# Hybrid block kernel: two of the four masked q/k halves of the upper head groups move from the end of the first head group to the second, and one q rounding is taken ahead of a fold

## The reference, cut to what matters

```
qkv = (layernorm(x) @ Wqkv + bqkv)            # 16 heads of 16 features
q = q*cos + rotate_half(q)*sin ; k likewise
scores = q @ k.T / sqrt(16), causal
out = softmax(scores) @ v
```

## Time and profile before

| what | value |
|---|---|
| median of three runs | 1737.48 us (1735.87 to 1737.56) |
| the profiled execution: span | 1734.1 us |
| the profiled execution's own time | not listed apart; the three runs lie 1.8 to 3.5 us above its span |
| busy share of the span | PE 95%, DVE 55%, ACT 42%, POOL 39% |
| chain that ended last | PE 78%, DVE 11%, ACT 6%, no visible cause 3%, POOL 1% |
| mean granted TensorE clock | 0.98 of full speed |

### The profile page before, as it was taken

One profiled execution on the slowest core, in us unless ns is written; L12 is line 12 of the kernel. 1 busy time (PEld: TensorE's weight loads), 2 busy tenths in 40 slices (PEclk: granted clock), 3 DMA queues, 4 the chain that ended last, 5 costly groups with the idle time before them and its releaser, 6 DMA issues.

```text
span 1734.1 us, 40451 instructions
## 1 busy us (share of the span) xinstructions
PE 1652.0 (95%) x17108; PEld 1186.6 (68%) x17108; DVE 952.4 (55%) x1978; ACT 722.2 (42%) x1510; POOL 670.1 (39%) x851
## 2 busy tenths in 40 slices
PE   6589999999999999999999999999999999999998
PEld 3467458864688547884588756886478855787477
DVE  6864657356553656546574565636565365744621
ACT  4433462334632455234633346233552346433441
POOL 5733335343542426324263433524353242733110
PEclk9779999999999999999999999999999999999999
DMA  5110000000000000000000000000000000000000
GB/s 184 51 50 13 1 14 3 1 25 13 3 2 6 20 13 3 2 25 1 14 3 1 25 14 2 3 0 25 13 3 2 13 13 1 4 2 0 1 13 13
DMA packets 20387, 25.77 MB, mean 15 GB/s; under 512 B 1488, under 2 KB 18800, under 8 KB 20208
## 3 DMA queue, kind: packets, MB, share of 16 engines
q1 hardware_dynamic: 19872, 22.13, 4.0%
q0 software_dynamic: 336, 1.05, 0.2%
HBM read 18.98 MB, written 4.19 MB: 13 GB/s over the span
## 4 chain that ended last, share of the span: by engine, by line
PE 78%; DVE 11%; ACT 6%; issue 3%; POOL 1%; DMA 1%; SPq 0%; DVEq 0%; POOLq 0%; ACTq 0%
PE ring L1592 19%; PE ring L1606 18%; PE ring L1752 6%; PE attn_out L1772 5%; PE ring L1578 5%; PE ring L1710 3%; PE ring L1538 3%; PE ring L1732 3%; PE ring L1645 3%; PE ring L1735 2%; PE ring L1530 2%; PE ring L1755 2%; PE ring L1615 2%; DVE x_z_xb L1176 1%; DVE big L1266 1%
## 5 line engine op out<-in xcount | busy, mean ns | idle before, releaser
L1333 DVE TENSOR_REDUCE maxes<-ring 128x2 f32<-128x1024 f32 (+5 forms) x290 | 197.5, 739 | 86.4 <-PE ring L1735 85.6
L757 POOL TENSOR_TENSOR rstd<-mean_var,eps_and_power 128x2 f32<-128x2 f32 x96 | 19.3, 201 | 470.0 <-DVE mean_var L1170 470.0
L1606 PE MATMUL ring<-w_down,big 128*128 128x256 f32 x784 | 175.9, 379 | 0.0
L1606 PEld LDWEIGHTS ring<-w_down,big 128*128 128x128 f32 x784 | 147.3, 190 | 19.6 <-issue 0.4
L809 POOL TENSOR_TENSOR big<-big,decay_blocks 128x256 f32<-128x256 f32 x192 | 141.5, 766 | 40.5 <-issue 35.9
L780 POOL TENSOR_TENSOR mix<-mix,z_t 128x512 f32<-128x512 f32 x80 | 85.7, 1100 | 117.8 <-DVE mix L1222 117.8
L1752 PE MATMUL ring<-big 32*128 32x512 f32 (+3 forms) x1024 | 124.6, 472 | 0.9 <-DVE big L1365 0.9
L1266 DVE TENSOR_TENSOR big<-big,decay_blocks 128x256 f32<-128x256 f32 x192 | 123.8, 671 | 1.0
L1024 ACT ACTIVATE big<-ring,up_bias 128x256 f32<-128x256 f32 x196 | 82.1, 470 | 101.3 <-PE ring L1592 101.3
L1592 PE MATMUL ring<-maxes,w_mlp 128*128 128x256 f32 x512 | 118.2, 385 | 0.0
L1592 PE MATMUL ring<-maxes,w_up 128*128 128x256 f32 x512 | 116.3, 381 | 0.7 <-ACT maxes L957 0.7
(11 more groups left out here) (202 smaller groups left out, 3250.1 us busy)
## 6 DMA issues: line engine op xcount, KB each, us to landing
x_in<-in_x SPq DMA_DIRECT2D x8, 512.0 KB, 3.8
delta<-in_x SPq DMA_DIRECT2D x7, 512.0 KB, 3.9
out<-x_z_xb SPq DMA_DIRECT2D x7, 512.0 KB, 2.9
w_mlp<-in_wm SPq DMA_DIRECT2D x2, 1024.0 KB, 6.3
w_mlp<-in_w_exp_t SPq DMA_DIRECT2D x1, 1028.0 KB, 9.1
v_ones<-in_w_con SPq DMA_DIRECT2D x1, 1024.0 KB, 10.1
w_mlp<-in_low_up SPq DMA_DIRECT2D x1, 1016.0 KB, 5.9
w_attention<-in_low_down SPq DMA_DIRECT2D x1, 1016.0 KB, 8.1
```

The source lines that it names most:

```text
L1333: nc.vector.tensor_reduce(maxes[:, t % 2, qt, 32 * gs[0] + row:32 * gs[-1] + row + 1:32], banks[:, first:last, lo:hi], AX_X, ALU.max).then ...
L1606: ins = mm(ps[:, a * D:(a + 1) * D], gelu(b, tag, m, t)[:, a * P:(a + 1) * P], wd[:, m, :], start=(m == 0), stop=(m == NF - 1))
```

## The change

The list of steps for elements 0 to 6 is changed in two places. At the end of group 0 only the q half of group 2 is left of the four halves, it and roundq 2 stand directly behind the fold of q, and the fold of k and roundk follow behind roundq 2. The k half of group 2 now stands in group 1 behind `E 1 a`, `divide 0` and `S 2 a`; the two halves of group 3 stand behind `E 1 b` and the "C" set (x5, blend, mix), ahead of `V 1 a`. No instruction is added or dropped, no wait is changed, and the order in which halves are counted stays the same. The branch for the last element is not touched.

```
@@ attention_steps, loop over t @@
-        o += fill[0] + [("E", t, "b")] + fill[1] + [("V", t, "a")]
+        o += [("half", 2, 1, "all")] if t == 1 else []
+        o += fill[0] + [("E", t, "b")] + fill[1]
+        o += halves(3) if t == 1 else []
+        o += [("V", t, "a")]
...
         if t == 0:
-            o += [("fold", 1, 0, "all"), ("fold", 1, 1, "all"), ("roundk", 1, "all")] + halves(2)
-            o += [("roundq", 2, "all")] + halves(3)
+            o += [("fold", 1, 0, "all"), ("half", 2, 0, "all"), ("roundq", 2, "all"), ("fold", 1, 1, "all"), ("roundk", 1, "all")]
```

## The result

The kernel after took 1756.14 us (median of four runs, 1753.37 to 1758.87) against 1737.13 us before; the ratio is 1.0106, 95% interval 1.0090 to 1.0122. The forecast was 1754.6 us in a range of 1747 to 1763. The profiled execution took 1756.46 us with a span of 1754.7 us, 20.6 us above the span of before.

The account below looks back on a forecast made before the run. PE was taken to bound the kernel, with 78% of the chain. Late blends of 11.9 us plus clock falls of 5.2 us made 17.1 us, on the 1737.5 us median 1754.6 us; range 1747 to 1763.

Parts of the forecast that it names:

- Move 1: Front of group 2 on ACT: three halves leave, k copy-out starts 2.0 us sooner and PE's bank wait goes.
- Move 2: POOL: roundq 2 before fold k and roundk; PE's group-2 maxima wait for roundk, net front gain 0.3 us per element.
- the upper bound of 0.6 to 0.9: Front of group 2: possible gain in us per element from both front moves if POOL is faster; 0.3 was taken.
- Move 3: Group 3's halves behind round b's exponentials: DVE's n = 3 blend waits, 1.70 us late per element, 11.9 us in all.
- The sign given for this move: DVE's C-set blend released by ACT, not PE's x5 matmuls, starting about 1.1 us behind round b's exponentials.
- The clock: PE's longer stall around rounds b and c: clock falls in four of seven elements, 1.3 us each, +5.2 us.
- rival 3: Stall in elements 0 to 6: clock falls in all seven, or for longer; 1758.5 us, up to 1767.6; chance 0.11.
- the forecast's case: Elements 0 to 6: blend late and clock falling in two to six of them, 1752 to 1757 us; chance 0.50.
- the waiting term: Elements 0 to 6: time lost to DVE's late blend, without clock falls; forecast as 11.9 us.

Follow-up runs that it names:

- e1: Against before: only group 2's q half stays in front, the other three halves go behind round a's exponentials, POOL's order unchanged; 1732.3 us, ratio 0.9967.
- f1: Against before: three halves behind round a's exponentials of group 1, with roundq 2 ahead of fold k and roundk on POOL; 1735.75 us, ratio 0.9985.
- e3: Against after: x5 matmuls and blends of the C set in order n = 0, 4, 3 instead of 3, 0, 4; 1740.5 us, ratio to before 1.0002.
- f3: Against after: the blend of n = 3 waits only for the group-3 half that reads what it overwrites; 1747.6 us, ratio to before 1.0052.
- e2: Against before: only group 3's two halves moved behind round b's exponentials, POOL's order kept; 1759.3 us, ratio 1.0105.
- e4: Against after: three extra matmuls at the head of group 1's round-c scores in elements 0 to 6; 1749.0 us, ratio to before 1.0054.
- f4: Against e2: the same kernel with the three extra matmuls of e4 in its stall; 1745.5 us, ratio to before 1.0045.

## Why the prediction was right

**Move 1 was right.** The copy-out stands at 609.83, behind one half, and is in no chain. e1 shows what this is worth when nothing else is changed: 0.94 us per element.

**Move 2 was right, to a tenth.** PE's group-2 maxima are released by POOL's roundk. Forecast was that the masks come 0.3 us earlier, counted from the first half; after has them at 612.77 - 609.00 = 3.77 us, before at 4.16, so 0.39, and f1 measured 0.40 for the stage. That POOL's order costs something against doing move 1 alone (0.53 us, f1 against e1) I had only as the upper bound of 0.6 to 0.9, if POOL were faster.

**Move 3 was right in mechanism and size.** The blends name ACT L1002, and the stage grew by 1.58 us where 1.70 was worked out; the total of 11.9 us was 11.1. The difference is the tenth by which the front did better: the blends start 619.73 - 609.00 = 10.73 us behind the first half, where 614.92 - 604.08 = 10.84 was worked out. The sign given for this move, a start 1.1 us behind the end of round b's exponentials, does not fit the prediction's own sum (614.92 - 613.57 = 1.35); measured was 619.73 - 618.39 = 1.34. e3 and f3 show that it is this wait: take it off the head of DVE's queue and 19.1 becomes 17.84, shorten it by a half and it becomes 18.44. e2 shows it without the POOL move.

**The clock was right in kind and too small.** I took four falls of 1.3 us, 5.2 us; it was five, one of them twice as long, 9.3 us together. Both factors were mis-sized. Counted in stretches of single length there were six and not four, which is 2.6 of the missing 4.1 us; the other 1.5 us is the price, since single falls cost 1.5 to 1.65 us here (19.15 to 20.65 or 20.80) and the long one 22.02 - 19.15 = 2.9. The 1.3 us came from a stage in which PE may have been held by other engines for part of the fall, while PE works densely at the end of this one. That reading was not tested, but one fall bears it out: in e2's element 4 it began early, 14.8 us behind the first copy, ahead of the last maxima's matmuls, which still wait for DVE, and cost 19.89 - 18.61 = 1.3 us; after's single falls began 15.8 to 17.2 us behind it.

The four was a choice between none and seven and not worked out, so that the forecast came within 1.5 us of the median run is in part luck. The profiled execution, to which the terms belong, lies 3.5 us above its sum (1754.7 against 1751.2): 4.1 us too little clock, 0.8 us too much wait, and 0.2 us elsewhere. That the falls belong to the stall was an inference from one row; e4 and f4 now show it.

**The rule on bank cycling.** The Trainium skill ("TensorE: Matmul & The Clock Gate", section "A second HAM failure mode: psum-queue depth-cycling") would have the clock swing at every such stage, which I priced as rival 3 at 1758.5 us. No trace here shows it in all seven elements: there are five in after and six in e2, both within the two to six of the forecast's case, and before has none at this place.

**The rule on gaps.** The Trainium skill ("Perfetto Trace Analysis", section "Optimization Strategy") tells one to find what the gap's instruction waits for and make that start sooner. By itself it was right: e1 does this and is faster. The loss came from where the moved work was put.

## What to carry to other kernels

When work is taken off a wait that bounds the kernel, look first for everything that waits for the moved work, also the buffer reuse of later work, and where that waiter stands in its engine's queue: here two halves that nobody read for microseconds held one DVE instruction, and eight more behind it. The free place is the one before the next user's inputs are ready (behind round a, 0.9 us gained per element), not the one where the engine is idle (behind round b, 1.6 us lost). And a stall of PE between narrow matmuls can cost as much again in clock; filling it with work is a quick way to see how much of a loss is clock.

## What the runs showed of the hardware that I had not expected

**A stalled PE looks busy in its matmul rows; its weight loads show the wait.** In element 2, the one that I used as the pattern, the stall has no idle time in PE's matmul rows. The round's matmuls, 0.71 us before, stand in after as one row of 2.67 us:

```profile
620.53 2.67 PE L1754 MATMUL ring<-big 32*128 32x256 f32 x8
```

So my remark that PE was busy 3.56 of 4 us before could not tell a free stage from a held one: a stretch of after of the same length, with the whole stall in it, gives 3.55.

```profile
620.50:624.50 4.00, 3.55 (x20) 1.71 (x16) 3.81 (x8) 1.03 (x4) 3.74 (x4) 1.00 0.00 0
```

Element 2 is the exception, though. In the six others PE's matmul rows do show 0.50 us of the wait, and in all seven the weight loads (PEld) name DVE each time, with more of it. In element 3:

```profile
827.20 2.01 PE L1754 MATMUL ring<-big 32*128 32x256 f32 x6
829.71 0.69 PE L1754 MATMUL ring<-big 32*128 32x256 f32 x2 [0.50 <-DVE maxes L1335]
```

```profile
827.20 0.29 PEld L1754 LDWEIGHTS ring<-big 32*128 32x128 f32 x2 [0.20 <-DVE mix L1224]
827.86 0.29 PEld L1754 LDWEIGHTS ring<-big 32*128 32x128 f32 x2 [0.37 <-DVE mix L1224]
828.51 0.29 PEld L1754 LDWEIGHTS ring<-big 32*128 32x128 f32 x2 [0.37 <-DVE mix L1224]
829.71 0.29 PEld L1754 LDWEIGHTS ring<-big 32*128 32x128 f32 x2 [0.90 <-DVE maxes L1335]
```

That is 0.20 + 0.37 + 0.37 + 0.90 = 1.84 us of waiting, for the blends and then for the maxima, as the prediction said (some 2 us per element). Summed over the whole execution (us in total, times, longest us), the weight loads of this line waited for DVE's blends and maxima 3.9 + 4.2 = 8.1 us before and 10.4 + 9.3 = 19.7 us after; the 11.6 us more are close to the 11.1 us of the waiting term.

```profile
PEld ring L1754 <- DVE mix L1224: 10.4, 33, 0.4
PEld ring L1754 <- DVE maxes L1335: 9.3, 16, 0.9
```

The page's PE busy time rose by 15.5 us, though PE had no more work; it holds waits and slow clock.

**Three more full-width matmuls in the stall kept the clock up.** With these (128x128 by 256 columns, 1.56 us in one row), falls went from five of seven to one (after, e4) and from six of seven to one (e2, f4), at no cost to the stage.
